# A two-layer graph network on one core: GpSimd's waits for landed gathers are placed by one condition instead of a table

## What is computed

```python
edge_index = jnp.stack([src, dst])
h = relu(layernorm(x))
x = x + (segment_sum(h[src], dst) @ W_rel.T + b_rel + h @ W_root.T)           # layer 0
h = relu(layernorm(x))
w = silu(edge_attr @ We1 + be1) @ We2 + be2                                   # layer 1
agg = segment_sum(h[src] * w, dst)
x = x + h + (silu(agg @ Wn1 + bn1) @ Wn2 + bn2)
```

## Time and profile before

| | |
|---|---|
| median of three runs | 4738.54 us |
| the profiled execution | 4729.43 us, span 4727.6 us |
| GpSimd busy | 2971.6 us, 63% |
| TensorE busy (matmul) | 2639.3 us, 56% |
| VectorE busy, ScalarE busy | 1009.6 us, 21%; 707.0 us, 15% |
| mean granted clock of TensorE | 0.694 of full speed |

### The profile page before, as it was taken

How to read it: one execution, slowest core, us unless ns; L and a number is a source line. 1 busy time by engine, 2 the same in 40 slices (tenths; PEclk the granted TensorE clock), 3 DMA queues, 4 the chain that set the end, 5 groups by cost and what they waited for, 6 DMA issues and landing times.

```text
span 4727.6 us, 35013 instructions
## 1 busy us (share of the span) xinstructions
PE 2639.3 (56%) x10150; PEld 1731.7 (37%) x10150; DVE 1009.6 (21%) x1790; ACT 707.0 (15%) x1212; POOL 2971.6 (63%) x3135
## 2 busy tenths in 40 slices
PE   1333333332333233233377778777787877878787
PEld 0232332232323233232334444444444444444444
DVE  2511111111111111111321222222222222222223
ACT  2400000000000000000121222222222222222222
POOL 5366666666666666666466666666666666666663
PEclk9765555565556555565676777777777877777788
DMA  4222222212221222212222222222222222222222
GB/s 131 67 53 52 53 59 53 55 52 52 55 59 52 52 60 54 53 52 54 64 64 64 66 67 66 63 66 72 65 67 67 66 70 67 67 67 65 66 70 60
DMA packets 230578, 296.71 MB, mean 63 GB/s; under 512 B 68707, under 2 KB 160277, under 8 KB 230432
## 3 DMA queue, kind: packets, MB, share of 16 engines
q0 software_dynamic: 100096, 205.20, 16.8%
q10 hardware_dynamic: 61378, 60.59, 4.6%
q1 hardware_dynamic: 69086, 30.73, 2.4%
HBM read 269.81 MB, written 26.48 MB: 63 GB/s over the span
## 4 chain that ended last, share of the span: by engine, by line
another core or an unknown queue 38%; PE 29%; issue 22%; DVE 6%; ACT 2%; DVEq 2%; POOL 1%; ACTq 0%; DMA 0%; SPq 0%; POOLq 0%
PE seg L381 8%; PE ew_a L381 4%; PE hid_b L423 3%; PE hid_a L428 3%; DVE onehot L748 2%; PE hid_b L428 2%; PE hid_c L423 2%; PE ew_b L434 2%; PE hid_a L423 2%; PE ew_a L434 1%; PE hid_c L428 1%; DVEq L756 1%; ACT hidden L605 1%; PE node L392 1%
## 5 line engine op out<-in xcount | busy, mean ns | idle before, releaser
L327 POOL DMA_INDIRECT rows<-h_rows,idx x3060 | 2906.3, 950 | 1671.7 <-issue 1248.4
L381 PE MATMUL seg<-onehot,rows 128*128 128x128 f32 x4784 | 897.1, 343 | 750.8 <-issue 419.9
L381 PEld LDWEIGHTS seg<-onehot,rows 128*128 128x128 f32 x4784 | 812.9, 252 | 841.2 <-issue 539.1
L381 PE MATMUL ew_a<-onehot,rows 128*128 128x128 f32 x1472 | 335.6, 358 | 763.2 <-issue 597.4
L381 PEld LDWEIGHTS ew_a<-onehot,rows 128*128 128x128 f32 x1472 | 282.6, 262 | 814.6 <-issue 765.6
L748 DVE TENSOR_TENSOR onehot<-iota_ps,dst_rel 128x1536 f32<-128x1536 f32 (+1 forms) x278 | 461.3, 1659 | 0.8 <-DVE dst_rel L736 0.6
L856 DVE TENSOR_TENSOR rows<-ew_a,rows 128x512 f32<-128x512 f32 x207 | 143.0, 691 | 843.4 <-remote 437.0
L760 DVE TENSOR_TENSOR agg<-seg,agg 128x128 f32 x207 | 60.4, 292 | 1108.9 <-remote 993.0
L856 DVE TENSOR_TENSOR rows<-ew_b,rows 128x512 f32<-128x512 f32 x184 | 127.0, 690 | 685.7 <-remote 343.2
L428 PE MATMUL hid_b<-hidden,we_sb 128*128 128x512 f32 x276 | 190.0, 776 | 86.1 <-ACT hidden L605 74.7
L428 PE MATMUL hid_a<-hidden,we_sb 128*128 128x512 f32 x278 | 219.0, 881 | 12.7 <-ACT hidden L605 10.8
(11 more groups left out here) (134 smaller groups left out, 1812.0 us busy)
## 6 DMA issues: line engine op xcount, KB each, us to landing
rows<-h_rows,idx POOLq DMA_INDIRECT x3060
ef_a<-ef_blocks ACTq DMA_DIRECT2D x70, 300.0 KB
node_work<-ef_blocks ACTq DMA_DIRECT2D x47, 300.0 KB
xs<-x SPq DMA_DIRECT2D x40, 256.0 KB
ys<-y_rows SPq DMA_DIRECT2D x26, 256.0 KB
out<-xs ACTq DMA_DIRECT2D x26, 256.0 KB
y_rows<-ys ACTq DMA_DIRECT2D x25, 256.0 KB
h_rows<-node_work ACTq DMA_DIRECT2D x23, 256.0 KB
```

Of the source, the lines that this page charges most:

```text
L327: pool.indirect_dma_start(out=rows[:, u, t, :], out_offset=None, in_=table, in_offset=bass.IndirectOffsetOnAxis(ap=idx[:, j:j + 1], axis=0 ...
L381: mm = pe.matmul(seg[layer][g % 2][:, 0:P], rows[:, u, t, :], onehot[:, g % 2, k * TB + t, :], start=(k == 0 and t == 0), stop=(last and t ...
```

## The change

The table `STOPS` and the line that reads it are taken out. The `hold` that stood under that line keeps its indentation, and by it now belongs to the condition above, `if g == HALF // GB`, which holds for group 3 alone.

```diff
@@ -30,7 +30,6 @@
 G = -(-U // GB)
 N_SUMS = ITERS * G
 assert G % 2 == 0 and HALF % GB == 0 and U == (G - 1) * GB + 2
-STOPS = ([2, 4], [1, 2, 3, 4, 5])
 H_SETS = 5
@@ -318,7 +317,6 @@
                         hold(pool, s_idx_a, loads * 16 + 16)
                     if g == HALF // GB:
                         hold(pool, s_idx_b, loads * 16 + 16)
-                    if g in STOPS[layer]:
                         hold(pool, s_rows[layer][g - 1], landed(i, g - 1))
                     hold(pool, s_seg[layer], i * G + (g + 1))
```

## The result

After the change the kernel takes 4781.48 us (median of four runs, 4774.62 to 4787.61) against 4733.99 us for the kernel before (four values, 4729.43 to 4745.97, of which 4729.43 stands twice): ratio 1.0096, interval 1.0069 to 1.0122. It is slower, as forecast, but by 47 us, where 152 us had been forecast. The profiled execution took 4744.91 us, 30 us less than the fastest of the four.

What follows compares the result with a forecast made beforehand. GpSimd's gathers and stops were taken to bound layer 1, with long gather runs holding TensorE back. Longer waits added 138 us in layer 1 and 24 in layer 0 to 4729, giving 4891, predicted as 4890 us; range 4780 to 5050.

Steps and rivals of the forecast that it cites:

- A stop costs 2.15 us, 247 us in all: GpSimd's removed stops, priced alone: four per iteration in layer 1 save 198 us, one in layer 0 saves 49 us.
- six pauses: GpSimd in a layer 1 iteration: five ahead of groups 1 to 5, one at the end, above 85.0 us of gathers.
- Unbroken gathers hold TensorE back: Both layers: TensorE crawls from about 10 us into a long gather run until it ends; pauses let it catch up.
- The first rival: Stops were pure cost in both layers: 4482 us in full, 4690 us in part; chance 0.23.
- The stops come back as waits at the same places: Main forecast: GpSimd's waits for TensorE's sums replace the stops and are longer, 4780 to 5100 us; chance 0.63.
- 6 us per iteration in layer 1: Net loss from longer waits in layer 1, taken near the shorter wait: 23 x 6 = 138 us.
- A wait behind 12 gathers: GpSimd in layer 1: 3.71 us idle against a stop's 2.43, 1.3 us more, 5 us per iteration over four places.
- A run of 24: Layer 1: 30 + 9.5 = 39.5 us for two groups that took 34.2; 14 us per iteration on 2.8 pairs.
- the crawl's rate: TensorE late in a gather run starts about half a matmul record per us, some 32 us per block.
- the crawl wins: Rival: layer 1's hand-overs get as late as layer 0's, an iteration takes about 120 us, 5190 us; chance 0.08.
- Layer 0, +1 us: Layer 0: one stop fewer saves 2.15 us, a longer wait for sums costs 3.2; 24 us over 23 iterations.
- The rule weighed against the reading: DMA engines alternate between queues packet by packet, so long gather runs should hold up no other queue for long.

Runs made afterwards that it cites:

- e14: No stops within an iteration in either layer, against the kernel before, where nothing holds TensorE back: 4151.17 us, ratio 0.9261.
- e9: Separate kernel, none of the reference computed: TensorE matmuls beside nothing, gathers, fills or direct DMAs in seven phases; 819.45 us where the kernel before took 4681.04 us.
- e16: Separate kernel, none of the reference computed: TensorE matmuls beside 68 gathers in seven patterns; 1087.39 us where the kernel before took 4680.08 us.
- e10: The kernel before, unchanged, profiled in a batch where nothing holds TensorE back: 4477.83 us, ratio 1.0.
- e7: The kernel before, unchanged, profiled in the same batch as e8: 4676.58 us, ratio 0.9996.
- e8: The changed kernel, profiled in the same batch as e7, against the kernel before: 4735.88 us, ratio 1.0124.
- e1: The changed kernel once more, against the kernel before at 4760.48 us in that batch: 4792.45 us, ratio 1.0068.
- e2: Layer 0 alone changed (one stop, ahead of group 3), layer 1 with its five stops, against the kernel before: 4757.83 us, ratio 0.9995.
- phase 2: Part of e16: gathers in runs of 12, each followed by a wait for its landing; 48 gathers and 258 matmul records in 70 us.
- e19: The kernel before with every stop kept, but waiting for only 11 of the 12 gathers ahead: 4813.93 us against 4751.73 us, ratio 1.0128.
- e15: The same separate kernel as e16, in a batch where nothing holds TensorE back: 698.83 us, 2.7 us per group of matmuls throughout.
- phase 1: Part of e16: 68 gathers issued unbroken beside TensorE's matmuls; 57 gathers and 42 matmul records in 70 us.

## Why the prediction was right in direction and wrong in size

- **A stop costs 2.15 us, 247 us in all.** Right where TensorE is free: seven stops fewer save 330 us (e14) of 346. The 14 us above 85.0 in an iteration were read as six pauses; 0.93 us of them lie ahead of the second gather of group 3 (1.23 us idle), where a stop and the wait for the indices stand together.
- **Unbroken gathers hold TensorE back.** Right for a held-back batch, and now shown rather than argued: in e9 and e16 TensorE waits for nobody within a phase. The first rival (stops are pure cost) is right in a free one, 0.9558. The waits for sums in layer 0, the oddest rows of before, are missing in e10; so that profile showed which kind it was, but not that the other kind exists. That the result was taken in a batch of the same kind is luck.
- **The stops come back as waits at the same places.** Right: the timeline above, and the expected look of it (runs of 12 and 24, none of 36). VectorE's adds wait longer, 292 us where it was 253 over the 2200 us. That the clock falls below 0.77 was wrong: it is 0.78. Nor do the matmuls of layer 1's sums get more spaced out: the idle time ahead of them in which nothing was waited for is 54 us before and 37 us after.
- **6 us per iteration in layer 1, the mis-sized term and the step that failed.** It is 0.60 us in the predicted pair, 0.65 us in e7 and e8, and 1.8 us in e1 and e2. Two pieces were too large. A wait behind 12 gathers was put at 3.7 us idle, from a row of layer 0, and is 3.0. A run of 24 was put at 9.5 us and is 4.4. The second came from the crawl's rate, half a matmul record per us, which I took from 128x128 sums of layer 0. In after's layer 1, TensorE starts 36 records in the late 18.5 us of the run of 24, 1.9 per us (second row; columns as above):

```profile
3629.00:3641.00 12.00, 12.00 (x40) 7.17 (x39) 2.55 (x4) 3.11 (x5) 8.38 (x9) 0.62 0.26 69
3641.00:3659.50 18.50, 11.83 (x36) 5.91 (x34) 2.76 (x4) 1.38 (x2) 14.15 (x15) 0.79 0.20 53
```

  And the pauses of before were not all plain stops. With TensorE already 20 to 56 tiles behind they average 2.66 us behind 12 gathers in layer 1, where e10 has 2.46.
- **Why the loss limits itself.** A rival (the crawl wins) asked if a wait for a sum brings the catch-up that a stop does. It does, since it too is a pause in the issuing. By the backlog reading the iteration cannot become much shorter than 68 gathers at the rate that TensorE bears, 68 x 70 / 48 = 99 us at phase 2's, an estimate. The held-back layers' 97 to 103 us lie around that with two stops, five or none; e19's 104.5 us lie above it. The stops neither gain nor lose much; they only say where the pause is.
- **Layer 0, +1 us.** It is 0.0 and +0.1 us per iteration, and e2 is 0.9995: no term.
- **The end of the kernel, missing.** The forecast had no term for it. TensorE a whole iteration behind was in the text (as the condition for the waits), but not that this work is left over behind the last gather. The omission is worth 41 of the 47 us in e7 and e8, where the stops had kept TensorE in step, but only 4.0 us in the predicted pair and 0.8 us between e1 and e2. So it is not what made the forecast too large.
- **The rule weighed against the reading.** The Trainium skill, DMA: Bandwidth & Descriptors, "Queues, rings and completion order", has each DMA engine take turns between its queues. My conclusion from it, that the unbroken runs cost nobody anything, agrees with e15 (629 records beside unbroken gathers) and not with e16 (42). What TensorE waits for in the crawl no profile here shows, so the rule may hold and the hold-up lie elsewhere.

No version beats both kernels everywhere: no stops is the fastest in a free batch (0.9261) and slower in a held-back one (1.0079). Open are what the backlog consists of, what TensorE waits for meanwhile (its instructions, its operands or its reports), and what makes a batch a held-back one. The record has a profile's span and clock for every execution, so whether TensorE is held back without a profiler beside it is open too.

## What to carry to other kernels

A stop that looks like pure idle time can be where another engine catches up. If that engine's records are spaced out with nothing in the program between them, price the stop at what comes back. Count also the work left over behind the last transfer, since an engine that is one iteration behind pays it once, at the end. It is a term only where the old kernel had kept that engine in step. And measure a change of this kind in more than one batch of runs: here its sign depended on it.

## What the hardware showed that I had not expected

- The same kernel takes 4479 to 4481 us in some batches, 4680 us in others and 4734 to 4760 us in the rest. In the first nothing in it or in the separate kernels is held back. In the other two the kernel with all its stops in layer 1 ends with TensorE 12 tiles behind (e7) and 52 to 58 (before, e2).
- TensorE crawls on for 10 us after the last gather of e16's phase 1, with the DMA engines at 4 GB/s.
- In a held-back batch 57 indirect gathers in 70 us leave TensorE 42 matmul records of 629, direct DMAs at 96 GB/s all of them. The passage is steep: 48 gathers leave 258, 46 leave 626.
- TensorE's reports are late with it. VectorE's mark of a finished group in e16's phase 1 came up to 70 us after the group's last matmul, against 0.1 us without gathers.
